# Softmax split of the second transformer block moved between engines

## The reference, cut to what matters

```python
h = film(rmsnorm(x, norm1_w), cond, film1_w, film1_b)
Q = h @ q_w + q_b;  K = h @ k_w + k_b;  V = h @ v_w + v_b
scores = jnp.einsum('bnd,bmd->bnm', Q, K) * D ** (-0.5)
attn = jax.nn.softmax(scores, axis=-1)
out = jnp.einsum('bnm,bmd->bnd', attn, V)
x = x_in + (out @ proj_w + proj_b)
h = film(rmsnorm(x, norm2_w), cond, film2_w, film2_b)
return x + (gelu(h @ mlp_w1 + mlp_b1) @ mlp_w2 + mlp_b2)
```

## Time and profile before

| what | value |
|---|---|
| median of 3 runs | 2288.89 us (2284.7 to 2292.79) |
| profiled execution, its own time | 2284.53 us |
| its span | 2282.7 us |
| PE, DVE, ACT, POOL busy | 89%, 69%, 50%, 32% |
| granted TensorE clock, mean | 0.958 of full |

### The profile page before, as it was taken

One profiled execution on the slowest core, in us unless ns is written; L12 is line 12 of the kernel. 1 busy time (PEld: TensorE's weight loads), 2 busy tenths in 40 slices (PEclk: granted clock), 3 DMA queues, 4 the chain that ended last, 5 costly groups with the idle time before them and its releaser, 6 DMA issues.

```text
span 2282.7 us, 40192 instructions
## 1 busy us (share of the span) xinstructions
PE 2029.6 (89%) x13491; PEld 1019.2 (45%) x13491; DVE 1581.3 (69%) x2821; ACT 1149.2 (50%) x2082; POOL 722.1 (32%) x661
## 2 busy tenths in 40 slices
PE   3867787989998999899988999899989999899889
PEld 3345333444444444444445444444445444444434
DVE  5678636887578756886588757886588757885422
ACT  4365544564448444555447444655457443754230
POOL 1153233442126402541135302622145212731121
PEclk8788898999999999899999999999999999999989
DMA  6632452212230213111230213121230223011212
GB/s 225 207 103 100 159 187 88 86 39 84 88 103 25 102 60 126 48 57 65 94 106 18 101 71 125 39 84 56 85 112 20 86 91 116 25 57 56 93 37 92
DMA packets 85523, 200.82 MB, mean 88 GB/s; under 512 B 7612, under 2 KB 48864, under 8 KB 73144
## 3 DMA queue, kind: packets, MB, share of 16 engines
q1 hardware_dynamic: 74920, 166.49, 21.7%
q10 hardware_dynamic: 10384, 31.49, 3.8%
HBM read 161.97 MB, written 35.72 MB: 87 GB/s over the span
## 4 chain that ended last, share of the span: by engine, by line
PE 55%; issue 17%; DVE 14%; ACT 7%; POOL 5%; DMA 1%; DVEq 0%; ACTq 0%; POOLq 0%; SPq 0%
PE banks L1368 11%; PE banks L1370 10%; PE banks L1369 10%; PE banks L1326 5%; PE banks L1261 4%; POOL memory L1193 3%; DVE memory L1144 3%; PE banks L1138 2%; PE banks L1047 2%; DVE memory L961 2%; PE banks L1208 2%; PE banks L1182 2%; PE banks L1243 1%; PE banks L1312 1%; DVE memory L976 1%
## 5 line engine op out<-in xcount | busy, mean ns | idle before, releaser
L1368 PE MATMUL banks<-memory 128*128 128x512 bf16 x1536 | 589.5, 384 | 32.3 <-DVE memory L1616 11.8
L1369 PE MATMUL banks<-memory 128*128 128x512 bf16 x1536 | 584.7, 381 | 0.0
L1370 PE MATMUL banks<-memory 128*128 128x512 bf16 x1536 | 584.6, 381 | 0.0
L1193 POOL TENSOR_TENSOR memory<-memory 128x512 bf16<-128x512 f32 x288 | 324.4, 1146 | 317.3 <-ACT memory L1189 316.0
L1144 DVE TENSOR_REDUCE memory<-banks 128x1 f32<-128x512 f32 x512 | 333.6, 680 | 47.0 <-PE banks L1138 44.4
L1189 ACT ACTIVATE memory<-banks 128x512 f32<-128x512 f32 x512 | 290.3, 596 | 138.9 <-PE banks L1182 137.6
L1594 POOL TENSOR_TENSOR memory<-memory 128x512 bf16<-128x512 f32 x128 | 144.6, 1132 | 583.3 <-DVE memory L1589 583.3
L1368 PEld LDWEIGHTS banks<-memory 128*128 128x128 bf16 x1536 | 149.3, 97 | 220.2 <-DVE memory L1616 19.3
L1138 PE MATMUL banks<-memory 96*128 96x512 bf16 x512 | 198.5, 411 | 52.9 <-DVE memory L1144 46.9
L1370 PEld LDWEIGHTS banks<-memory 128*128 128x128 bf16 x1536 | 148.9, 97 | 187.5 <-issue 5.6
L1369 PEld LDWEIGHTS banks<-memory 128*128 128x128 bf16 x1536 | 152.3, 99 | 165.6 <-issue 5.0
(11 more groups left out here) (175 smaller groups left out, 2880.3 us busy)
## 6 DMA issues: line engine op xcount, KB each, us to landing
memory<-weight_parts SPq DMA_DIRECT2D x80, 1024.0 KB, 4.9
memory<-head_parts SPq DMA_DIRECT2D x192, 128.0 KB, 2.8
head_parts<-memory SPq DMA_DIRECT2D x64, 256.0 KB, 2.8
weight_parts<-memory ACTq DMA_DIRECT2D x10, 1024.0 KB, 4.9
memory<-in_x SPq DMA_DIRECT2D x32, 256.0 KB, 3.3
memory<-ada_rows SPq DMA_DIRECT2D x16, 512.0 KB, 4.5
memory<-in_L_cond_w_fc ACTq DMA_DIRECT2D x2, 4096.0 KB, 14.2
memory<-in_L_cond_mlp_w ACTq DMA_DIRECT2D x8, 1024.0 KB, 8.4
```

The lines of the kernel that those rows point to most:

```text
L1193: eng.tensor_tensor(prob_lo[:, e % RING], expo[:, e % RING], prob_hi[:, e % RING], ALU.subtract).then_inc(ok.sem, 1)
L1368: pe.matmul(bank, lh, rh, start=(k == 0), stop=False)
L1369: pe.matmul(bank, lh, rl, start=False, stop=False)
L1370: mm = pe.matmul(bank, ll, rh, start=False, stop=(k == KC - 1))
```

## The change

What it does, in seven points:

1. pT(t): the fp32 probabilities are no longer turned. Their high half is the upper 16 bits of each fp32 word, read in place (`p1_halves`); POOL computes the low half into a new buffer `p1_low` (`p1_rest`); PE turns both halves as bf16, eight 128x128 transposes into one bank, the four low ones behind a wait on POOL; ACT copies the 128 x 1024 bf16 result in one instruction (`p_copy`), which frees the bank. DVE's subtraction (L1549) is gone.
2. proj(t): ACT scales the product by the reciprocal of the sum into y1 and frees the bank (`proj_scale1`); POOL adds it to x1 (`proj_add1`). DVE keeps the reciprocal. The squares wait for POOL's add.
3. The late q and k of chunk 2 (`QK_POOL`): ACT writes the biased fp32 value back in place, a second instruction in `qk_high`, and POOL subtracts (`qk_rest`) in place of DVE's `qk_low`. Chunks 0, 1 and 3 stay on DVE.
4. pT0 moves from ahead of slot (0, 0) to slot (0, 1); pT1 to pT3 stay at (0, 3), (0, 10), (0, 15) on PE. ACT's reads are at (0, 1), (0, 3), (0, 12), (0, 15), where they were ahead of the slots and at (0, 2), (0, 11), (0, 14).
5. POOL's order becomes: the residual biases, p1_rest(0), value_low 0 and 1, p1_rest(1), value_low 2 and 3, qk_rest(q), p1_rest(2), qk_rest(k), p1_rest(3), then proj_add1 of tiles 0 to 2 ahead of its first `prob_low`, that of tile 3 ahead of the seventh.
6. proj's reads move from DVE's table to ACT's, at the same slots (0, 15), (0, 22), (0, 23), (1, 5).
7. The wait for the stores of the sample before moves from the squares to `proj_scale1`.

```diff
-PT_AT, PT_READ = (((0, 3), (0, 10), (0, 15)), ((0, 2), (0, 11), (0, 14)))
+PT_AT, PT_READ = (((0, 1), (0, 3), (0, 10), (0, 15)), ((0, 1), (0, 3), (0, 12), (0, 15)))
+POOL_AT = (0, 0, 0, 6)
+QK_POOL = (("q", 2), ("k", 2))
...
+        p1_low = big[:, 6 * T:7 * T].bitcast(BF16).rearrange("p (r n) -> p r n", r=2)
...
+                if (name, c) in QK_POOL:
+                    act.wait_ge(hi_ok.sem, hi_ok(i, 2 * c + a + 1))
+                    act.activation(qk_f[:, a], qk_f[:, a], ACT.Identity, bias=bias).then_inc(qk_sum.sem, 1)
+        def qk_rest(pool, i, c, part):
+            a = "qk".index(part)
+            pool.wait_ge(parts_out.sem, parts_out(i, 32 * c))
+            pool.wait_ge(qk_sum.sem, qk_sum(i, QK_POOL.index((part, c)) + 1))
+            pool.tensor_tensor(part_lo[:, a], qk_f[:, a], part_hi[:, a], ALU.subtract).then_inc(lo_ok.sem, 1)
...
+        def p1_halves(t):
+            return wide[:, t % 2].bitcast(BF16).rearrange("p (n s) -> p n s", s=2)[:, :, 1], p1_low[:, t % 2]
+        def p1_rest(pool, i, t):
+            done(pool, plan1, ("s", t), i)
+            if t >= 2:
+                ready(pool, plan1, ("pT", t - 2), i)
+            else:
+                all_done(pool, plan0, [("fc2", TT - 1)], i)
+            high, low = p1_halves(t)
+            pool.tensor_tensor(low, wide[:, t % 2], high, ALU.subtract).then_inc(p1_lo.sem, 1)
         def turn_p1(pe, i, t):
             done(pe, plan1, ("s", t), i)
             b = take(pe, plan1, ("pT", t), i)
-            for k in range(TT):
-                mm = pe.transpose(banks[:, b, k * P:(k + 1) * P], wide[:, t % 2, k * P:(k + 1) * P], ident)
+            out = banks[:, b].bitcast(BF16).rearrange("p (s k n) -> p s k n", s=2, k=TT)
+            for s, part in enumerate(p1_halves(t)):
+                if s == 1:
+                    pe.wait_ge(p1_lo.sem, p1_lo(i, t + 1))
+                for k in range(TT):
+                    mm = pe.transpose(out[:, s, k], part[:, k * P:(k + 1) * P], ident_bf)
             mm.then_inc(full[b].sem, 1)
-        def p_high(act, i, t): ...
-        def p_low(dve, i, t): ...
+        def p_copy(act, i, t):
+            b = ready(act, plan1, ("pT", t), i)
+            act.activation(act_k[:, :, :, t * P:(t + 1) * P],
+                           banks[:, b].bitcast(BF16).rearrange("p (s k n) -> p s k n", s=2, k=TT), ACT.Copy
+                           ).then_inc(free[b].sem, 1)
-        def proj_add1(dve, i, t): ...
+        def proj_scale1(act, i, t):
+            b = ready(act, plan1, ("proj", t), i)
+            act.wait_ge(inv1.sem, inv1(i, t + 1))
+            act.wait_ge(out_done.sem, out_done(i, 0))
+            act.activation(y1[:, t], banks[:, b], ACT.Copy, scale=suminv1[:, t:t + 1]).then_inc(free[b].sem, 1)
+        def proj_add1(pool, i, t):
+            done(pool, plan1, ("proj", t), i)
+            pool.wait_ge(x1_bias.sem, x1_bias(i, t + 1))
+            pool.tensor_tensor(x1[:, t], x1[:, t], y1[:, t], ALU.add).then_inc(x1_sum.sem, 1)
```

POOL's stream in `both`:

```diff
+                if j is not None:
+                    p1_rest(pool, j, 0)
+                if i is not None:
+                    for t in range(2):
+                        value_low(pool, i, t)
+                if j is not None:
+                    p1_rest(pool, j, 1)
+                if i is not None:
+                    for t in range(2, TT):
+                        value_low(pool, i, t)
+                    for part, late in QK_POOL[0:1]:
+                        qk_rest(pool, i, late, part)
+                if j is not None:
+                    p1_rest(pool, j, 2)
+                if i is not None:
+                    for part, late in QK_POOL[1:2]:
+                        qk_rest(pool, i, late, part)
+                if j is not None:
+                    p1_rest(pool, j, 3)
```

More of the change, by code:

```diff
@@ L133 @@
 LOW_AT = {(0, 17): 0, (1, 11): 1, (2, 11): 2, (3, 12): 3}
+POOL_AT = (0, 0, 0, 6)
+QK_POOL = (("q", 2), ("k", 2))
 EXTRA_DVE = (17, 22, 25, 30, 34, 38)
-LOW_DVE = [e for e in range(KC * HEADS) if e >= FIRST_DVE or e in EXTRA_DVE]
+EXTRA_POOL = ()
+LOW_DVE = [e for e in range(KC * HEADS) if (e >= FIRST_DVE or e in EXTRA_DVE) and e not in EXTRA_POOL]
 LOW_POOL = [e for e in range(KC * HEADS) if e not in LOW_DVE]
@@ L376, in two_blocks @@
         nmax1_ok = signal("nmax1_ok", 12)
+        p1_lo = signal("p1_lo", TT)
+        qk_sum = signal("qk_sum", max(1, len(QK_POOL)))
+        x1_sum = signal("x1_sum", TT)
         inv1 = signal("inv1", 4)
-        pT_hi = signal("pT_hi", 4)
         g1_hi = signal("g1_hi", 16)
@@ L1082, in qk_high @@
                     act.wait_ge(parts_out.sem, parts_out(i, 32 * c))
-                act.activation(part_hi[:, a], qk_f[:, a], ACT.Identity,
-                               bias=bias_cols[:, a * KC + c:a * KC + c + 1]).then_inc(hi_ok.sem, 1)
+                bias = bias_cols[:, a * KC + c:a * KC + c + 1]
+                act.activation(part_hi[:, a], qk_f[:, a], ACT.Identity, bias=bias).then_inc(hi_ok.sem, 1)
+                if (name, c) in QK_POOL:
[6 more added lines that the diff above has]
+            pool.tensor_tensor(part_lo[:, a], qk_f[:, a], part_hi[:, a], ALU.subtract).then_inc(lo_ok.sem, 1)
         def spill_parts(sp, i, c):
@@ L1375, in squares1 @@
             rows, normed = ((x0, y), (x1, y1))[a]
-            if a == 1:
-                act.wait_ge(out_done.sem, out_done(i, 0))
             for t in tiles:
-                done(act, *((plan0, ("fc2", t)) if a == 0 else (plan1, ("proj", t))), i)
+                if a == 0:
+                    done(act, plan0, ("fc2", t), i)
+                else:
+                    act.wait_ge(x1_sum.sem, x1_sum(i, t + 1))
                 act.activation(normed[:, t], rows[:, t], ACT.Square, scale=float(D) ** -0.5,
@@ L1635, in two_blocks @@
         s_p = lambda s_at, p_at: [(at, ("s", t + 2)) for t, at in enumerate(s_at)] + [
-            (at, ("pT", t + 1)) for t, at in enumerate(p_at)]
+            (at, ("pT", t)) for t, at in enumerate(p_at)]
         PE_AT = place(*s_p(S_AT, PT_AT), *((at, ("proj", t)) for t, at in enumerate(PROJ_AT)),
                       *((at, ("turn", k)) for k, at in enumerate(TURN_AT)), *((at, (*M[k // KC], (k % KC,))) for k, at in enumerate(M_AT)))
-        DVE_AT = place(*s_p(S_AT, PT_READ), *((at, ("proj", t)) for t, at in enumerate(PROJ_READ)),
+        DVE_AT = place(*s_p(S_AT, PT_READ),
                        *((later(at, 2), ("low", k)) for k, at in enumerate(TURN_AT)))
-        ACT_AT = place(*s_p(S_AT, PT_READ), *((at, ("square", t)) for t, at in enumerate(SQUARE_AT)),
+        ACT_AT = place(*s_p(S_AT, PT_READ), *((at, ("proj", t)) for t, at in enumerate(PROJ_READ)), *((at, ("square", t)) for t, at in enumerate(SQUARE_AT)),
                        *((at, ("norm", t)) for t, at in enumerate(NORM_AT)),
@@ L1739, in both @@
                         e = c * HEADS + n
+                        if j is not None:
+                            for t, at in enumerate(POOL_AT):
+                                if e == at:
+                                    proj_add1(pool, j, t)
                         if i is not None and e in LOW_POOL:
@@ L1776, in highs1 @@
                         elif name == "pT":
-                            p_high(act, j, *at)
+                            p_copy(act, j, *at)
+                        elif name == "proj":
+                            proj_scale1(act, j, *at)
                         elif name == "fc1":
@@ L1942, in lows1 @@
                         elif name == "pT":
-                            p_low(dve, j, *at)
-                        elif name == "proj":
                             invert1(dve, j, *at)
-                            proj_add1(dve, j, *at)
                         elif name == "fc1":
@@ L2013, in both @@
                     value_full(dve, i)
[L2014 removed]
+                lows1(j, [("s", 1)])
                 for c, n in slots():
@@ L2027, in both @@
                             part, late = LATE_LOW[c, n]
-                            qk_low(dve, i, late, part)
+                            if (part, late) not in QK_POOL:
+                                qk_low(dve, i, late, part)
                         if (c, n) in LOW_AT:
@@ L2185, in both @@
                     v_product(pe, i)
-                products1(j, [("s", 1), ("pT", 0)])
+                products1(j, [("s", 1)])
                 if j is None:
```

13 lines of the change are left out of this document (2 added, 11 removed).

## The result

The changed kernel takes 2328.2 us (median of 4 runs, 2325.25 to 2329.83) against 2287.0 for the kernel before: ratio 1.018, 95% interval 1.0161 to 1.0199. I had forecast slower, by 16 us and within 2274 to 2318; it is 41. The direction and the place were right, the size was not.

What follows compares the result with a forecast made beforehand. It took PE's matmuls in a row as the main bound, with DVE bounding c = 0. Seven passes 11.9, last pass 1.4 and clock 3 made 16 us slower; it named 2303 us, range 2274 to 2318.

Steps and rivals of the forecast that it cites:

- Slots 0 to 15: Up to proj0: late q and k ahead of p1_rest on POOL hold PE at pT2 and pT3; proj0 3.8 us later.
- From proj0 to c = 1: Between proj0 and the first score of c = 1: 10.0 us instead of 11.3, so c = 1 begins 2.5 late.
- The clock: Behind two new PE gaps in every pass: more falls to 1.2 GHz, 3 us in all, bounds -5 and +12.
- much slower: Rival, chance 0.15: the forecast's chain, clock falls in every pass, and POOL and DVE collisions in c = 1; +29, 2316.
- Its other term: In c = 1, within the rival "much slower": POOL and DVE collisions cost 1 us a pass.
- c = 1: Heads after the scores start: POOL's idle of 2.4 us absorbs part of the delay, leaving 1.7 us a pass.
- POOL without gaps: Sign in the changed profile: POOL has no gaps from the first low part until the fourth head.
- Prices: Instruction times on ACT and POOL: copy of pT about 1.06 us, p1_rest 1.04, qk_rest 1.08, proj_add1 1.09.
- The last pass: No slots there: tail after proj3 +1.1 us and twice +0.15 before pT1 and pT3, 1.4 in all.
- Faster: Rival, chance 0.24: DVE bounds c = 0 and loses 7.3 us a pass, so 11 us less, 2275.

Runs made afterwards that it cites:

- e3: Changed kernel with filler on PE, useless repeat transposes in its waits at pT1 to pT3: 2306.7 us, ratio 1.0077 to the kernel before.
- e10: Changed kernel with only pT3's low half put ahead of k's late subtraction on POOL: 2306.5 us, ratio 1.0098 to the kernel before.
- e11: Changed kernel with only pT2's low half put ahead of q's late subtraction on POOL: 2305.9 us, ratio 1.0095 to the kernel before.
- e1: Changed kernel with the low halves of pT2 and pT3 ahead of the late q and k on POOL: 2283.3 us, ratio 0.9978 to the kernel before.
- e7: Kernel before with only proj's scale moved to ACT and its add to POOL: 2284.8 us, ratio 1.0000.
- e8: Changed kernel with POOL's order of e1 and proj's scale and add back on DVE: 2280.0 us, ratio 0.9989 to the kernel before.
- e9: Kernel of e8 with ACT's read of pT2 at (0, 8), not (0, 12): 2278.8 us, ratio 0.9969 to the kernel before.

## Why the prediction was right in its place and wrong in its size

**Slots 0 to 15: right.** The chain through POOL's order was worked out to gaps of 2.2 and 3.0; they are 2.28 and 2.46. k's product was to start 17.7 us after the exp (664.9) and starts at 17.80. proj0 was to be 3.8 late; it is 3.80 in e3 at full clock and 4.17 in the changed kernel. e10 and e11 confirm both halves of the chain, and e1 that without it the loss is gone.

**From proj0 to c = 1: right at full clock, wrong in the kernel.** I took 10.0 us up to PE's first score of c = 1, DVE's waits being gone. In e3, at full clock, it is 9.97 in every pass. In the changed kernel it is 10.9 to 12.6, because the clock is at 1.2 GHz in this stretch.

**The clock: the step that failed.** It reads "If falls come in all seven passes and not in about half, it costs 3.5 x 2.6 = 9; I take a third of it, 3." It measures about 21 in all (2328.2 less 2306.7 of e3). Three things were wrong in it. The falls do come in all seven passes, so there was nothing to take a third of. Some passes have one more: three of the seven have a fall 7 or 17 us after the exp, and proj0 then starts 1.5 to 1.7 later. And the price of 2.6, from two passes of before, was read without asking where it is paid. A changed pass takes 4.0 to 6.1 more than the 254.3 of a pass of e3 at full clock. Before, the fall near 20 us after the exp cost 1.2 by proj0's end, which comes 23.8 us after the exp (417.17) and 22.6 without the fall (669.80), but only 0.24 at c = 1: in the pass without the fall PE waits there for DVE, for 0.52 and 0.45. PE of the kernel before, the first row from the pass of 393.36, the others from that of 647.23:

```profile
417.17 0.60 PE L1138 MATMUL banks<-memory 96*128 96x512 bf16 x2
...
670.92 0.60 PE L1151 MATMUL banks<-memory 128*4 128x128 f32 x4 [0.52 <-DVE memory L1144]
672.39 0.39 PE L1138 MATMUL banks<-memory 96*128 96x512 bf16 x1 [0.45 <-DVE memory L1144]
```

Nearly all of the 2.6 belonged to the falls 53 and 67 us after the exp, in c = 2: in these two passes the fourth head is 0.24 apart (53.11 and 52.87 after the exp), the eighth 2.7 (74.15 and 71.44). In the changed kernel those waits for DVE are gone, and the falls cost 1.0 to 2.6 between proj0 and c = 1 (10.9 to 12.6 against 9.97). The rival "much slower", which had the falls in every pass, put them at 9 and ended at 2316, still too low. Its other term, 1 us a pass for POOL and DVE in each other's way in c = 1, doesn't show: POOL's low parts (L1210) take 1164 ns in the mean, against 1146 before.

**c = 1: wrong.** I let POOL's idle of 2.4 absorb the delay, so that 2.5 late became 1.7. In e3 c = 1 begins 2.5 late, as forecast, but the fourth head is 2.7 late. Measured from PE's first score of c = 1 to the fourth head, the time is 21.6 before and 21.7 to 21.8 in e1, e3, e7, e8 and the changed kernel, whatever POOL has ahead. The stage gives nothing back; POOL without gaps was no sign that it was the bound there. With this, a pass at full clock costs 3.0 (254.3 in e3 against 251.3), not 1.7, and seven passes 21, not 12: the second term that was mis-sized.

**Prices.** ACT's copy of 1024 elements 1.02 (I took 1.06), p1_rest 1.04, qk_rest 1.09, the second write 0.72: right. proj_add1 takes 1.27, not the 1.09 of L1408. The last pass was to cost 1.4 and costs 2.3 (from its first exp to the end: 130.4 against 128.1).

**The rivals.** "Faster" rested on DVE as the bound of c = 0. DVE's relief was real (7.85 to 6.27 us of the 8), and in e1 the waits for DVE between proj0 and c = 1 went as forecast: 9.98 us against 11.28 before. Ahead of proj0 it bought almost nothing. PE waits for DVE for 0.29, 0.21 and 0.81 in e1 and for 0.43, 0.21 and 0.81 at the same slots before, because in e1 DVE had itself waited 2.06 us for PE, which waited for POOL's half at pT1. And proj0 starts 0.3 later than before because of the 0.76 for ACT's copy of pT2; with that copy moved, in e9, it starts 0.5 earlier. In two passes of e1 at full clock up to there, c = 1 begins 1.0 earlier than before and the fourth head is 0.8 earlier, but these passes take 252.0 and 252.2, not less than 251.3, with a fall of the clock 70 us after the exp, which takes about 1.0 back (13.1 us from the eighth to the twelfth head before, 14.1 here). So DVE's busy share was in part backlog: the relief is worth 1.0 us where c = 1 begins, and of the time of e1 it leaves 0.2% (interval 0.04 to 0.40%).

## What to carry to other kernels

When work moves to an engine that is mostly idle, look at its order first: an instruction that waits holds all behind it, and each new pair of jobs has to be checked for the one whose input comes last. Two moves that each cost nothing may cost 2% together. And idle time of PE can have a second price, a lower clock, where a long run of products follows; read the duration of the matmuls behind a gap, not only the gap. A fall of the clock cost 0.24 us where PE would have waited for DVE anyway, and 1.0 to 2.6 in the same stretch without those waits.

## What the runs showed of the hardware

- Behind a gap of 2.46 us ahead of pT3 and one of 2.28 before it the matmuls take 0.63 instead of 0.38 us; with PE kept at useless transposes over the same time, the granted clock is 1.00 over the first 30 us of every pass and the kernel gains about 21 us. Over the seven passes the mean granted clock is 0.97 in the changed kernel, 0.98 before, and 0.99 with filler.
- POOL's add of two fp32 tiles takes 1.27 us in the new `proj_add1` (L1598) and 1.09 when one operand is a bias row (L1426, 1093 ns). What makes the difference was not tried.
- ACT's copy of 128 x 1024 bf16 out of PSUM takes 1.02 us, where 512 elements take 0.59: less than two copies (1.18), and no gain from bf16 input, since 512 elements of bf16 take as long as of fp32 (L1335 of the changed kernel 596 ns, L1543 of the one before 590).
